# Small constant bf16 products on TensorE inside the attention walks of a graph network

## The chip, the cores and the metric

The kernel runs on one core of one Trainium2 chip. The metric is the device time of one execution in microseconds (us), taken as the median of several executions. The profile is one further execution, recorded by the hardware profiler; its span runs from the first to the last recorded instruction.

## The reference

Four layers run one after the other over 3125 nodes with 256 features, each a graph attention followed by a feed-forward part with experts, each added to `x`. The change touches the graph attention of layer 0, layer 1 and layer 2 (there twice, called l2a and l2b below). All of them compute, over 50,000 edges sorted by target node and with 8 heads:

```
h = einsum('nd,dhf->nhf', x, W)
logits = leaky_relu(al_s[src] + al_d[dst], 0.2)     # al_s, al_d: 8 numbers for each node
m = segment_max(logits, dst)
e = exp(logits - m[dst])
out = segment_sum(h[src] * e, dst) / (segment_sum(e, dst) + eps)
```

In l2a and l2b each node also has an edge to itself. Layer 3's attention and all the feed-forward parts have loops of their own and are not touched.

## The kernel before

`gat_layer` (line 1207) normalizes and transposes the nodes, projects them (`project`), and calls `gat_edges` (line 597), the walk over the edges. It is called four times: l0, l1, l2a, l2b; in the profile's names the digits of l0 and l1 are left out, so that both are `l_edges`.

A walk takes the edges in 416 tiles of 128, in 26 chunks (`NCK`) of 16 tiles (`CK`), each chunk in four groups (`GR` = 4 tiles). For a tile, `stage` holds the gathered rows of the source nodes (256 features, their 8 ones and 8 logits of the source). A product of a one-hot matrix `hotT` with `adn` gives every edge the logits of its target node (the **expansion**, line 856, into `ps_ad`); a product of the one-hot matrix `hot` with the weighted rows `msg` sums the edges of each target node (the **scatter**, line 890, into `ps_sum`), and DVE adds the sum to `acc` (line 764), one tile at a time. The softmax runs with a running maximum: the logits of a chunk are turned (line 863), scanned on DVE, the ends of the tiles and the tops of the chunk are passed through two small products (lines 867 and 872), the maxima are turned back (line 877), and the first block's sums are rescaled (line 753, with the product of line 881).

Each engine has its own program, and semaphores tie them. All of it is software-pipelined: while chunk c is scattered, the maxima of chunk c + 1 are made.

- **POOL** (line 653) issues one indirect gather for a tile. From the third chunk on, a group's gathers wait for `msg_built` of the same group two chunks before, since `stage` has two halves.
- **SP** (line 661) loads the rows for `hotT`.
- **DVE** in a chunk (line 768): `weigh` (line 745, makes `msg` of one group), `rescale`, the logits of the next chunk (lines 677 to 685, which need `ps_ad`), then three times `weigh` and a step of the maxima with four adds between its instructions (lines 691 to 697, 705 to 714, 722 to 730), then `hotT` of chunk c + 2 (line 672), `exponents` (lines 738 and 739, which need the turned maxima) and the last four adds.
- **ACT** makes `hot` (lines 812, 815), the weights (line 828), and in l2a and l2b the own weights (line 820).
- **PE** in a chunk (line 892): scatter of group 0, turn of the logits; scatter 1, `place_ends`; scatter 2, `place_tops`; scatter 3, the block numbers of chunk c + 2 into registers, `turn_maxima`, `place_f`, and the expansion of chunk c + 2. A scatter's product waits until DVE has added what `ps_sum` of the same number held (`added`).

The walk uses the eight PSUM banks: four `ps_sum`, `ps_ad`, `ps_p`, `ps_x` (the turned logits, and in its first columns `ps_f`) and `ps_y` (turned maxima, `ps_ends`, `ps_init`). All of the operands of its products are f32.

## Time and profile before

| | us |
|---|---|
| median of 3 runs | 7869.34 (7864.52 to 7906.43) |
| span of the profiled execution | 7089.8 |
| PE busy | 5426.1 (77%) |
| DVE busy | 4048.3 (57%) |
| POOL busy | 2934.6 (41%) |
| ACT busy | 2394.9 (34%) |
| mean granted TensorE clock | 0.796 of full |

The median lies 779.5 us over the span: that much lies around the first and the last recorded instruction. The busy shares are means over stages with different limits; the walks stand at about 210 to 860, 1500 to 2150, 2520 to 3170 and 3265 to 3920 us of the span.

In the rows below, PE is TensorE's products, PEld its weight loads, which overlap them. A clock of 1.00 is 2.4 GHz and 0.50 is 1.2 GHz. An f32 product appears as two records of each kind, so that 16 expansions are 32 records and the four products of one scatter are 8. A record's own duration includes the time in which it overlaps its neighbours; the pace is read from starts.

### The profile page before, as it was taken

How to read it: one execution, taken by the hardware profiler on the slowest of the kernel's cores; microseconds unless marked ns; L12 is line 12 of the kernel's file. 1: busy time of each engine (PE TensorE's matmuls, PEld its weight loads, DVE VectorE, ACT ScalarE, POOL GpSimd, SP SyncE). 2: the span in 40 equal slices, each digit the busy share in tenths (PEclk: the TensorE clock that was granted, in tenths of full speed). 3: DMA queues.
4: the chain of work that ended last, by engine and by line, in shares of the span. 5: the costliest groups of instructions: out<-in, count | busy, mean ns of one | idle time of the engine just before them, and what ended most of it. 6: DMA issues, size and time to landing. Idle time of an engine off the chain costs nothing. (4 is left out here: it accounts for less than half of the span.)

```text
span 7089.8 us, 85054 instructions
## 1 busy us (share of the span) xinstructions
PE 5426.1 (77%) x21265; PEld 3965.8 (56%) x21266; DVE 4048.3 (57%) x8410; ACT 2394.9 (34%) x5747; POOL 2934.6 (41%) x2894
## 2 busy tenths in 40 slices
PE   0788759458886678875888488888979998476998
PEld 0566436346664555654666344446768887354776
DVE  5466733356664447764777577762147776794112
ACT  0333212123332133332333255542205554362333
POOL 1566432336660056644666277760007776000000
PEclk9666659766667866766766699998989999796999
DMA  3433323233440044433334111110019999461000
GB/s 89 124 115 116 70 79 110 80 93 114 117 103 12 2 123 114 117 93 98 115 115 100 41 30 32 31 19 18 7 48 345 353 357 254 120 196 16 9 13 23
DMA packets 455428, 710.74 MB, mean 100 GB/s; under 512 B 105113, under 2 KB 334039, under 8 KB 455015
## 3 DMA queue, kind: packets, MB, share of 16 engines
q0 software_dynamic: 142432, 380.88, 19.8%
q1 hardware_dynamic: 310442, 318.36, 14.1%
q10 hardware_dynamic: 2304, 8.52, 0.3%
q8 instruction: 114, 1.87, 0.1%
q14 instruction: 136, 1.11, 0.1%
HBM read 604.94 MB, written 102.97 MB: 100 GB/s over the span
## 5 line engine op out<-in xcount | busy, mean ns | idle before, releaser
L653 POOL DMA_INDIRECT l_edges_stage<-l_h_rows,src_t x832 | 831.9, 1000 | 463.5 <-issue 238.9
L890 PE MATMUL l_edges_ps_sum<-l_edges_msg,l_edges_hot 128*128 128x264 f32 x1664 | 741.2, 609 | 172.2 <-DVE l_attn_acc L764 157.1
L2086 POOL DMA_INDIRECT l_edge_kv<-l_kv_rows,src_t x416 | 465.1, 1118 | 741.0 <-POOLq L1999 557.2
L2522 POOL DMA_INDIRECT l_gate_edges_srow<-l_gate_src_rows,l_gate_edges_idx x512 | 567.6, 1109 | 251.4 <-issue 155.8
L890 PEld LDWEIGHTS l_edges_ps_sum<-l_edges_msg,l_edges_hot 128*128 128x128 f32 x1664 | 446.4, 291 | 373.2 <-DVE l_attn_acc L764 276.9
L2656 PE MATMUL l_gate_edges_ps<-l_gate_edges_wide,l_gate_edges_hot_lo 128*128 128x500 f32 x1024 | 487.0, 633 | 127.3 <-DVE l_gate_edges_wide L2584 127.3
L653 POOL DMA_INDIRECT l2a_edges_stage<-l2a_h_rows,src_t x416 | 414.0, 995 | 236.8 <-issue 114.7
L653 POOL DMA_INDIRECT l2b_edges_stage<-l2b_h_rows,src_t x416 | 413.2, 993 | 237.4 <-issue 116.8
L890 PE MATMUL l2b_edges_ps_sum<-l2b_edges_msg,l2b_edges_hot 128*128 128x272 f32 x832 | 355.3, 581 | 87.6 <-DVE l2b_attn_acc L764 79.8
L890 PE MATMUL l2a_edges_ps_sum<-l2a_edges_msg,l2a_edges_hot 128*128 128x272 f32 x832 | 353.9, 579 | 87.6 <-DVE l2a_attn_acc L764 77.7
L2656 PEld LDWEIGHTS l_gate_edges_ps<-l_gate_edges_wide,l_gate_edges_hot_lo 128*128 128x128 f32 x1024 | 204.9, 205 | 369.6 <-issue 214.5
L764 DVE TENSOR_TENSOR l_attn_acc<-l_attn_acc,l_edges_ps_sum 128x264 f32 x832 | 350.4, 421 | 79.4 <-DVE l_attn_acc L764 34.1
L2187 PE MATMUL l_edge_ps_e<-l_edge_w,l_edge_eaT 128*128 128x256 f32 x1664 | 377.0, 380 | 0.0
L2307 DVE SCALAR_TENSOR_TENSOR l3f_acc<-l_experts_psb,l3f_g,l3f_acc 128x256 f32<-128x256 f32 x200 | 96.8, 484 | 444.7 <-PE l_experts_psb L2338 444.6
L2187 PEld LDWEIGHTS l_edge_ps_e<-l_edge_w,l_edge_eaT 128*128 128x128 f32 x1664 | 317.8, 191 | 43.9
L890 PEld LDWEIGHTS l2b_edges_ps_sum<-l2b_edges_msg,l2b_edges_hot 128*128 128x128 f32 x832 | 204.1, 271 | 198.0 <-DVE l2b_attn_acc L764 153.7
L2368 ACT ACTIVATE l_experts_hT<-l_experts_psa,l_experts_sc_pair 128x320 f32<-128x320 f32 x320 | 197.5, 617 | 343.3 <-PE l_experts_psa L2329 323.3
L890 PEld LDWEIGHTS l2a_edges_ps_sum<-l2a_edges_msg,l2a_edges_hot 128*128 128x128 f32 x832 | 201.7, 268 | 198.5 <-DVE l2a_attn_acc L764 155.6
L2584 DVE TENSOR_TENSOR l_gate_edges_wide<-l_gate_edges_hot_hi,l_gate_edges_val 128x500 f32<-128x500 f32 x512 | 307.6, 674 | 6.4
L1133 PE MATMUL l_agg_ps<-l_agg_msg,l_agg_hot 128*128 128x264 f32 x832 | 209.0, 409 | 82.8 <-DVE l_attn_acc L1098 69.2
L856 PE MATMUL l_edges_ps_ad<-l_attn_adn,l_edges_hotT 128*128 x1664 | 250.2, 291 | 28.2 <-DVE l_edges_hotT L672 28.2
L2613 ACT ACTIVATE l_gate_edges_hot_lo<-col,l_gate_edges_nlo 128x128 f32<-128x128 f32 x512 | 156.4, 388 | 338.0 <-PE l_gate_edges_ps L2656 338.0
(745 smaller groups left out, 11376.6 us busy)
## 6 DMA issues: line engine op xcount, KB each, us to landing
l_val_rows<-l_edge_vj SPq DMA_DIRECT2D x104, 512.0 KB, 5.7
l_agg_stage<-l_val_rows SPq DMA_DIRECT2D x52, 1024.0 KB, 5.3
l_edge_ea<-in_edge_attr SPq DMA_DIRECT2D x388, 128.0 KB, 5.1
l_edges_rel_b<-rel_rows SPq DMA_DIRECT2D x52, 512.0 KB, 4.0
l_experts_w<-in_L_ffn_w SPq DMA_DIRECT2D x32, 512.0 KB, 4.6
l_gate_edges_lo_b<-l_gate_edges_lo_rows SPq DMA_DIRECT2D x64, 256.0 KB, 3.2
l_edges_stage<-l_h_rows,src_t POOLq DMA_INDIRECT x832, 2.8
l2a_edges_rel_b<-rel_rows SPq DMA_DIRECT2D x26, 512.0 KB, 4.0
```

The lines of the kernel that those rows point to most:

```text
L653: nc.gpsimd.indirect_dma_start(out=stage[:, c % 2, u, :], out_offset=None, in_=h_rows, in_offset=bass.IndirectOffsetOnAxis(ap=K.src_t[:, c ...
L764: nc.vector.tensor_tensor(to, to, ps_sum[u][:], ALU.add).then_inc(added, 1)
L856: last = nc.tensor.matmul(ps_ad[:, u, :], hotT[:, u * P:(u + 1) * P], adn[:, bass.ds(blks[u], 1), :].rearrange("p a h -> p (a h)"), start= ...
L890: nc.tensor.matmul(ps_sum[u][:], hot[:, g, u, :], msg[:, g % 2, u, :], start=True, stop=True).then_inc(summed, 1)
L1133: nc.tensor.matmul(ps[u][:], hot[:, n % 2, u, :], msg[:, n % 2, u, :], start=True, stop=True).then_inc(summed, 1)
L2086: nc.gpsimd.indirect_dma_start(out=kv[:, m, u, :], out_offset=None, in_=kv_rows, in_offset=bass.IndirectOffsetOnAxis(ap=K.src_t[:, n * EB ...
L2187: last = nc.tensor.matmul(ps_e[h][:, u, :], eaT[:, n % ES, 2 * h + u, c, :], w[:, c, :], start=(c == 0), stop=(c == DC - 1))
L2368: nc.scalar.activation(hT[l][:, v % 2, f, half * HALF:(half + 1) * HALF], psa[n % NA][:], ACT.Relu, bias=sc_pair[:, 1, l, v // NG, f:f + 1 ...
L2522: nc.gpsimd.indirect_dma_start(out=srow[:, n % 4, u, :], out_offset=None, in_=src_rows, in_offset=bass.IndirectOffsetOnAxis(ap=idx[:, n * ...
L2584: nc.vector.tensor_tensor(wide[:, s, u], bcast(hot_hi[:, n % 3, u, :], GV), val[:, s, u, :].unsqueeze(1).to_broadcast([P, NT, GV]), ALU.mu ...
L2613: nc.scalar.activation(hot_lo[:, s, u, :], K.col[:], ACT.Abs, bias=nlo[:, n * GB + u:n * GB + u + 1]).then_inc(near_lo, 1)
L2656: nc.tensor.matmul(flat, hot_lo[:, n % 2, u, :], wide[:, n % 2, u].rearrange("p t f -> p (t f)"), start=False, stop=False).then_inc(summed, 1)
```

## The change

A constant tile `warm` of ones in bf16 (128 x 256) is set once. `keep_warm(n)` issues n products of its first 128 columns with all 256, into a PSUM bank that nobody reads. PE issues two of them ahead of each of the 16 tiles of an expansion, and five after each of the four scatters of a chunk (after the small product that follows the scatter for groups 0 to 2, and ahead of the last small products for group 3). That is 32 + 20 in a chunk. To free a bank, `ps_x` and `ps_y` become one bank `ps_w` with separate columns for all five small results, and `place_f`, whose result no longer lies over the turned logits, goes ahead of `turn_maxima`. No wait is added or removed.

```diff
--- before.py
+++ after.py
@@ -133,6 +133,7 @@
                 nc.gpsimd.iota(col_i[:], [[1, P]], base=0, channel_multiplier=0).then_inc(iota_set, 1)
                 nc.gpsimd.iota(row_i[:], [[1, 1]], base=0, channel_multiplier=1).then_inc(iota_set, 1)
                 nc.gpsimd.memset(K.izero[:], 0).then_inc(ident_set, 1)
+                nc.gpsimd.memset(K.warm[:], 1.0)
 
             @block.vector
             def _(dve):
@@ -491,6 +492,7 @@
         self.ones = sb("ones", [P, P])
         self.col = sb("col", [P, P])
         self.row = sb("row", [P, 1])
+        self.warm = sb("warm", [P, 2 * P], BF16)
         self.izero = sb("izero", [P, BATCH], U32)
         self.rel_t = sb("rel_t", [P, STEPS])
         self.bad_t = sb("bad_t", [P, STEPS])
@@ -629,10 +631,10 @@
         ps_sum = [ph.psum(f"ps_sum{u}", [P, MW]) for u in range(GR)]
         ps_ad = ph.psum("ps_ad", [P, CK, AW])
         ps_p = ph.psum("ps_p", [P, CK, HEADS])
-        ps_x = ph.psum("ps_x", [P, P])
-        ps_y = ph.psum("ps_y", [P, P + 2 * CK + 2])
-        lgT, ps_f = ps_x[:], ps_x[:, 0:HEADS]
-        maxT, ps_ends, ps_init = ps_y[:, 0:P], ps_y[0:HEADS, P:P + 2 * CK], ps_y[:, P + 2 * CK:P + 2 * CK + 2]
+        ps_w = ph.psum("ps_w", [P, 2 * P + 2 * CK + 2 + HEADS])
+        ps_warm = ph.psum("ps_warm", [P, 2 * P])
+        lgT, maxT, ps_ends = ps_w[:, 0:P], ps_w[:, P:2 * P], ps_w[0:HEADS, 2 * P:2 * P + 2 * CK]
+        ps_init, ps_f = ps_w[:, 2 * P + 2 * CK:2 * P + 2 * CK + 2], ps_w[:, 2 * P + 2 * CK + 2:]
 
         rel_in = [ph.sem(f"rel_in{m}") for m in range(2)]
         gathered = [ph.sem(f"gathered{m}") for m in range(2)]
@@ -848,11 +850,16 @@
 
             @block.tensor
             def _(pe):
+                def keep_warm(n):
+                    for _ in range(n):
+                        nc.tensor.matmul(ps_warm[:], K.warm[:, 0:P], K.warm[:], start=True, stop=True)
+
                 def expand(c, m, blks):
                     pe.wait_ge(hotT_built, c + 1)
                     if not (isinstance(c, int) and c == 0):
                         pe.wait_ge(lg_made, c)
                     for u in range(CK):
+                        keep_warm(2)
                         last = nc.tensor.matmul(ps_ad[:, u, :], hotT[:, u * P:(u + 1) * P],
                                                 adn[:, bass.ds(blks[u], 1), :].rearrange("p a h -> p (a h)"), start=True, stop=True)
                     last.then_inc(expanded, 1)
@@ -893,18 +900,22 @@
                     scatter(c, 0)
                     if after >= 1:
                         turn_logits(c + 1, 1 - m)
+                    keep_warm(5)
                     scatter(c, 1)
                     if after >= 1:
                         place_ends(c + 1)
+                    keep_warm(5)
                     scatter(c, 2)
                     if after >= 1:
                         place_tops(c + 1)
+                    keep_warm(5)
                     scatter(c, 3)
                     if after >= 2:
                         blks = block_ids(nc, mybir.EngineType.PE, K, c + 2)
+                    keep_warm(5)
                     if after >= 1:
+                        place_f(c + 1)
                         turn_maxima(c + 1)
-                        place_f(c + 1)
                     if after >= 2:
                         expand(c + 2, m, blks)
 
@@ -913,8 +924,8 @@
                 turn_logits(0, 0)
                 place_ends(0)
                 place_tops(0)
+                place_f(0)
                 turn_maxima(0)
-                place_f(0)
                 expand(1, 1, block_ids(nc, mybir.EngineType.PE, K, 1))
                 with pe.Fori(0, NCK // 2 - 1) as j:
                     for m in range(2):
```

## Rows read from the trace of the kernel before

**Rows 1.** The page's parts 1 and 2: span, PE busy, granted clock

```profile
span 7089.8 us, 85054 instructions
...
PE 5426.1 (77%) x21265; PEld 3965.8 (56%) x21266; DVE 4048.3 (57%) x8410; ACT 2394.9 (34%) x5747; POOL 2934.6 (41%) x2894
...
PEclk9666659766667866766766699998989999796999
```

**Rows 2.** Groups by line: count, busy us, mean ns, idle before

```profile
L890 PE MATMUL l_edges_ps_sum<-l_edges_msg,l_edges_hot 128*128 128x264 f32 x1664 | 741.2, 609 | 172.2 <-DVE l_attn_acc L764 157.1 <-DVE l_edges_msg L745 7.1
...
L653 POOL DMA_INDIRECT l_edges_stage<-l_h_rows,src_t x832 | 831.9, 1000 | 463.5 <-issue 238.9 <-DVE l_edges_msg L745 148.3 <-POOLq L528 76.3
```

**Rows 3.** Line 753 without its first run, in layer 0 and l2a

```profile
L753 DVE SCALAR_TENSOR_TENSOR l_attn_acc<-l_edges_ps_x,l_attn_acc x25: 426/433/434, 274.1 to 845.6; 128x264 f32 x25
...
L753 DVE SCALAR_TENSOR_TENSOR l2a_attn_acc<-l2a_edges_ps_x,l2a_attn_acc x25: 426/433/434, 2583.2 to 3159.9; 128x264 f32 x25
```

**Rows 4.** Gathers: l2a's group by line; landing in layers 0 and 1

```profile
L653 POOL DMA_INDIRECT l2a_edges_stage<-l2a_h_rows,src_t x416 | 414.0, 995 | 236.8 <-issue 114.7 <-DVE l2a_edges_msg L745 84.6 <-POOLq L528 37.5
...
DMA to landing us min/median/max: 2.7/2.8/5.2
```

**Rows 5.** Sum and mean of twelve stretches of 25 us, l2a

```profile
sum 300.00, PE 259.39 PEld 184.80 DVE 217.09 ACT 111.84 POOL 197.55; mean PE 21.62 PEld 15.40 DVE 18.09 ACT 9.32 POOL 16.46
```

**Rows 6.** Stretches of 1 us: busy PE, PEld, DVE, ACT, POOL, PEclk, DMA

```profile
2728.50:2729.50 1.00, 1.00 (x6) 1.00 (x6) 0.00 (x0) 0.00 (x0) 0.69 (x2) 0.50 0.50 139
...
2742.50:2743.50 1.00, 0.21 (x1) 0.21 (x2) 0.86 (x3) 0.00 (x0) 0.70 (x2) 1.00 0.52 139
...
2747.50:2748.50 1.00, 1.00 (x9) 1.00 (x9) 0.79 (x3) 0.76 (x3) 0.76 (x1) 0.78 0.82 262
...
606.90:607.90 1.00, 1.00 (x12) 1.00 (x11) 0.96 (x2) 1.00 (x4) 0.00 (x0) 1.00 0.60 229
...
607.90:608.90 1.00, 1.00 (x7) 1.00 (x7) 0.99 (x2) 0.97 (x3) 0.10 (x1) 0.50 0.01 4
...
615.90:616.90 1.00, 1.00 (x3) 0.77 (x3) 1.00 (x2) 0.00 (x0) 0.69 (x2) 0.50 0.32 83
```

**Rows 7.** Time order, one chunk of l2a: start, us, engine, line, idle before

```profile
2722.77 0.29 DVE L738 TENSOR_TENSOR l2a_edges_own_x<-l2a_edges_own,l2a_edges_ps_y 128x128 f32<-128x128 f32 x1 [0.63 <-PE l2a_edges_ps_y L877]
...
2723.19 7.01 PE L856 MATMUL l2a_edges_ps_ad<-l2a_attn_adn,l2a_edges_hotT 128*128 x32
...
2726.69 0.43 DVE L753 SCALAR_TENSOR_TENSOR l2a_attn_acc<-l2a_edges_ps_x,l2a_attn_acc 128x264 f32 x1
...
2730.03 3.98 PE L890 MATMUL l2a_edges_ps_sum<-l2a_edges_msg,l2a_edges_hot 128*128 128x272 f32 x8
...
2730.34 0.29 DVE L677 TENSOR_TENSOR l2a_edges_z<-l2a_edges_stage,l2a_edges_ps_ad 128x128 f32<-128x128 f32 x1 [3.22 <-PE l2a_edges_ps_ad L856]
...
2734.37 0.42 DVE L691 TENSOR_TENSOR_SCAN l2a_edges_local<-cuts_f,l2a_edges_ps_x 128x128 f32<-128x128 f32 x1 [1.68 <-PE l2a_edges_ps_x L863]
...
2735.17 2.54 PE L890 MATMUL l2a_edges_ps_sum<-l2a_edges_msg,l2a_edges_hot 128*128 128x272 f32 x8 [0.95 <-DVE l2a_attn_acc L764]
...
2743.29 2.88 PE L890 MATMUL l2a_edges_ps_sum<-l2a_edges_msg,l2a_edges_hot 128*128 128x272 f32 x8 [0.81 <-DVE l2a_attn_acc L764]
...
2746.71 0.32 PE L877 MATMUL l2a_edges_ps_y<-ident,l2a_edges_seg_max 128*128 128x128 f32 x1 [0.54 <-issue]
```

**Rows 8.** The same view, one chunk of layer 0

```profile
604.95 4.34 PE L856 MATMUL l_edges_ps_ad<-l_attn_adn,l_edges_hotT 128*128 x32
...
609.14 3.87 PE L890 MATMUL l_edges_ps_sum<-l_edges_msg,l_edges_hot 128*128 128x264 f32 x8
...
613.37 0.42 DVE L691 TENSOR_TENSOR_SCAN l_edges_local<-cuts_f,l_edges_ps_x 128x128 f32<-128x128 f32 x1 [2.17 <-PE l_edges_ps_x L863]
...
628.25 0.34 PE L877 MATMUL l_edges_ps_y<-ident,l_edges_seg_max 128*128 128x128 f32 x1
```

**Rows 9.** Line 856 alone while the clock is full, layer 0

```profile
L856 PE MATMUL l_edges_ps_ad<-l_attn_adn,l_edges_hotT x26: 256/256/277, 604.9 to 607.8; 128*128 x26
```

## The prediction

> **What bounds the kernel now.** I read the page's totals first [rows 1]: the span is 7089.8 us, PE is busy for 77% of it, and its clock line shows 6s and 7s where the attention layers run, so TensorE often has half of its clock there. A sum over 7 ms says nothing about four loops of 600 us, so the next view is the costliest groups [rows 2]: the scatter product (line 890) and the gathers (line 653) of `gat_edges` are at its top, and with the expansion (line 856) they are the work of the four walks. The starts of the one rescaling per chunk (line 753) give their pace [rows 3]: in layer 0, 25 of the 26 lie from 274.1 to 845.6 us, 23.8 us a chunk, and in l2a from 2583.2 to 3159.9, 24.0. The first one is left out: it stands some 32 us before the second, in both, because the first gathers are still being issued. Layer 1 keeps the pace of layer 0, and l2b that of l2a.
>
> Three engines could set that pace. POOL: 416 gathers of l2a take 414 us busy, 114.7 us of issue between them, and 84.6 us in which POOL waits for `msg` [rows 4]. Its own work is therefore (414 + 114.7) / 26 = 20.3 us a chunk. It has some 3.5 us to spare. DVE is busy for 18.1 of every 25 us [rows 5], and waits for PE at three places: for `ps_ad` (3.22 us), for the turned logits (1.68 and 2.17 us) and for the turned maxima (0.63 us) [rows 7, 8]. PE is busy for 21.6 of every 25 us [rows 5]. So the loop is PE and DVE handing work to each other, and in the long hand-overs PE is late.
>
> Now the clock, microsecond by microsecond [rows 6]. In l2a the scatters of groups 1 to 3 run at 1.00 (2.4 GHz), though PE is idle for about 1 us ahead of each (0.95 and 0.81 ahead of the first and the last [rows 7]). The expansion begins half a microsecond after 2746.71 us, and in the microsecond from 2747.5 the mean is down to 0.78 with PE busy 1.00; the level it falls to is 0.50 (1.2 GHz), as in the chunk before. It stays there through expansion and scatter 0, and scatter 1 has the full clock again: 2.54 us against 3.98 [rows 7]. In layer 0 the expansion starts at 1.00, falls at about 607.9 in its midst, and the scatters are mostly at 0.50. What goes before a fall is thus seldom idleness: it is the stretch of expansions, weight loads with products of 8 or 16 columns.
>
> **The change, part by part.** Walk the chunk from one expansion's start to the next, and price it with the full clock everywhere.
>
> (a) Expansion, 16 tiles. In layer 0, 26 records start in 2.8 us at the full clock [rows 9], 0.108 us each, 0.216 a tile of two records; at half clock 32 take 6.9 us, 0.43 a tile [rows 7]. The change puts two bf16 products of 256 columns ahead of each tile. No row shows such a product. One column a cycle gives 256 / 2.4 GHz = 0.107 us, and 0.213 at half clock; that is the low end. The nearest row, a scatter record of 264 or 272 columns in f32, takes 3.98 / 8 = 0.50 us at half clock [rows 7], so 0.25 at full: it passes its columns twice, and is the high end. I take 0.107, since a 16-bit operand has no need of the second pass. If the first f32 weight load lies wholly beside the second of them, a tile costs 0.216 + 0.214 - 0.107 = 0.32 us; if nothing overlaps and their own two loads (half an f32 load each) show too, 0.54. Loads lie beside products in the scatters, but a filler's load behind a tiny product has no cover, so I take 0.40: 6.4 us an expansion, from 5.2 to 8.6. Against 4.34 us (layer 0 [rows 8]) and 6.9 (l2a) that is +2.1 and -0.5 us.
>
> The Trainium skill (TensorE: Matmul & The Clock Gate, section Back-to-back issue gap) states columns / 2.4 GHz plus 2.5 ns, 0.109 us for this product; no run here shows it yet, and by it the sum would be the same within 0.1 us a chunk.
>
> (b) From the expansion's end to the first scan over the turned logits (line 691). In layer 0 that is 609.29 to 613.37 us, in l2a 2730.15 to 2734.37 [rows 7, 8], nearly all of it scatter 0 at half clock (3.87 and 3.98 us) and the turn. At full clock the scatter takes 1.95 us, and the DVE's own work there (line 677 to the end of `weigh`) takes about 2.0 to 2.4, which is next late. The stretch shrinks from 4.1 and 4.2 us to 2.4 and 2.5: -1.7 us in both.
>
> (c) From there to the turn of the maxima (line 877). In l2a at full clock: 2734.37 to 2746.71, 12.34 us, paced by DVE's adds, which PE waits for [rows 7]. In layer 0, mostly at half clock: 613.37 to 628.25, 14.88 us [rows 8]. At full clock layer 0 should fall to the same 12.34: -2.5 us there, 0 in l2a. Three sets of five fillers (0.54 us each) fall into this part, ahead of scatters 1, 2 and 3, where PE is idle for 0.81 us at the least [rows 7]. They cost nothing at full clock; at half clock (1.07 us) they would show by up to 0.3 us each.
>
> (d) The fourth set stands between scatter 3 and the last small products, where nothing covers it: +0.54 us. `place_f` now goes ahead of `turn_maxima`; the two take the same time together, so the expansion starts no later by it, but the DVE's exponents come 0.3 to 0.4 us later. Who waits for that: the last four adds, `weigh` of the next group 0 and through it POOL. From the exponents (line 738, 2722.77) to line 677 (2730.34 less its wait of 3.22) is 4.35 us of DVE work [rows 7], under the 6.4 us of the expansion, so it is covered; without that cover it would be 0.4 us a chunk.
>
> (e) The rest: merging the small results into one PSUM bank adds no wait, since the order of their writers and readers stands; the memset of `warm` is once. The added weight loads and products (52 pairs a chunk) go through PE's queue alone; SP and POOL get nothing.
>
> Sum for a chunk: layers 0 and 1, 2.1 - 1.7 - 2.5 + 0.54 = -1.6 us, to about 22.3; l2a and l2b, -0.5 - 1.7 + 0.54 = -1.7 us, to about 22.4. Times 24 chunks and two walks each: 77 + 82 = 159 us. Against the profiled execution: 7089.8 - 159 = 6931 us of span. The median of the runs, 7869.34, lies 779.5 us over that span; what lies around the span doesn't change, so the forecast is 7869 - 159 = 7710 us, 2.0% less.
>
> What could stop it earlier: POOL. A gather waits for `weigh` of the chunk two before, and the next logits wait for the last gather to land (2.8 us [rows 4]). From line 677 to the end of the following `weigh` would be 2.4 + 12.34 + 1.1 + 3.9 us (the last from 2722.77 to the rescaling at 2726.69 [rows 7]), 19.7 in all; with 3.8 for the last gather and its landing and 15 x 1.27 for the gathers between, two chunks take 42.6 us: 21.3 us is the least for a chunk. 22.3 is above it, but little more is to be had.
>
> **Rivals.** (A) The fillers don't hold the clock through the expansion. For it: it falls there today with PE busy the whole time, and why it falls is only inferred. Against it: what falls is the stretch of tiny products, and the fillers bring 512 columns a tile; scatters with idle gaps between them keep the full clock in l2a. Price, if nothing changes in the clock: in l2a a tile costs 0.80 us, the expansion 12.8 (+5.9), the last fillers 1.07, the gaps 0.4: +7.3 us a chunk. In layer 0, 2.9 us at full clock do seven tiles and nine take 7.0: 9.9 (+5.6), with the rest +7.0. Times 48 each: +690, 8550 us; if the scatters gain the clock and only the expansions lose it, some 8250. I take 8400. The change decides at an expansion of about 6.4 + 1.65 = 8.0 us, 0.50 a tile: dearer than that and it is slower.
>
> The Trainium skill (same page, section HAM oscillation — how this bites in real kernels) ties the fall to idle gaps longer than any within these walks. The trace disagrees: 0.50 with PE busy 1.00 [rows 6]. By that rule fillers in short gaps would change nothing in the clock, and their cost would stay: rival A's 8550 us.
>
> (B) The clock holds, but fillers are dear (about 0.50 us a tile, no overlap, sequencer time for four instruction pairs a tile): expansion 8.0 us, no gain: 7870 us. (C) They are cheap (0.33 a tile) and POOL's 21.3 us becomes the bound: gains of 2.5 and 2.7 us, 48 times each, 250 us: 7620 us.
>
> **How the numbers follow.** Forecast 0.52, (C) 0.16, (B) 0.14, (A) 0.18. The low end is (C) with 20 us to spare, 7600. The high end takes in (B) and the mild edge of (A), 7960; what lies beyond is most of (A), under 2 in 10. A measurement of this kernel can tell 0.5% (39 us) from no change. Faster by more: 0.52 + 0.16 less a little = 0.67; within: 0.13; slower: 0.20.
>
> **What would show it.** Right: the granted clock at 0.9 to 1.0 all through the walks, in the expansions above all; 32 fillers and 32 expansion records in about 6.4 us; scatter 0 in about 2.0 us; line 753 every 22.3 to 22.4 us; POOL's wait for `msg` down from 84.6 us to about 40 in l2a; PE busier, near 0.9. Wrong: the clock still at 0.50 in an expansion, or an expansion over 8 us at full clock, or chunks under 21.3 us.

## The result and the profile after

The change made the kernel slower. Its median is 8166.59 us (8149.32 to 8170.57) beside 7880.51 us (7864.52 to 7906.43) for the kernel before (the runs of the 7869.34 above and one more), a ratio of 1.036 [1.033, 1.040]. The forecast was 7710 us, 2.0% faster, and its range ended at 7960.

The first view is the page of the kernel after: span, busy time of each engine, granted clock in 40 slices (it answers [rows 1]).

```profile
span 8168.8 us, 95871 instructions
...
PE 5570.9 (68%) x26673; PEld 4090.1 (50%) x26674; DVE 4044.2 (50%) x8410; ACT 2391.9 (29%) x5747; POOL 2871.8 (35%) x2895
...
PEclk9787768867787867778677877888898999788899
```

Two things stand in it. This execution's own time was 8170.57 us, so what lies around its span is 1.8 us, not 779.5. And its span is 1079 us over that of the shown profile of before [rows 1], though its clock line is higher (mostly 7s and 8s in the walks, where before has 6s and 7s), DVE, ACT and POOL are busy for as long as they were, and PE for only 145 us more. The time went into waiting, and far more of it than the two medians are apart.

The costliest groups (instruction count, busy us, mean ns, then the idle time before them and what ended it; they answer [rows 2, 4]):

```profile
L655 POOL DMA_INDIRECT l_edges_stage<-l_h_rows,src_t x832 | 818.6, 984 | 937.0 <-DVE l_edges_msg L747 630.3
L897 PE MATMUL l_edges_ps_sum<-l_edges_msg,l_edges_hot 128*128 128x264 f32 x1664 | 593.9, 503 | 539.0 <-DVE l_attn_acc L766 457.9
...
L655 POOL DMA_INDIRECT l2a_edges_stage<-l2a_h_rows,src_t x416 | 402.6, 968 | 488.3 <-DVE l2a_edges_msg L747 336.9
...
L855 PE MATMUL l_edges_ps_warm<-warm 128*128 128x256 bf16 x2704 | 475.2, 284 | 41.0 <-DVE l_edges_hotT L674 28.7
```

The scatters of layers 0 and 1 take 594 us of PE where they took 741 [rows 2]: the clock gain is there. But POOL, which was to wait 40 us for `msg` in l2a, waits 337 us. The pace of the rescaling in layer 0 (line 755, which was 753; the columns are as in [rows 3]) shows how much slower the loop turns:

```profile
L755 DVE SCALAR_TENSOR_TENSOR l_attn_acc<-l_edges_ps_w,l_attn_acc x25: 427/432/434, 302.7 to 1075.5; 128x264 f32 x25
```

That is 772.8 us for 24 chunks, 32.2 us each, against 23.8 [rows 3] and a forecast of 22.3. The waits of DVE and POOL in the walk of l2a name the place (who <- what it waited for: us in total, times, longest us):

```profile
POOL l2a_edges_stage L655 <- DVE l2a_edges_msg L747: 336.9, 46, 14.7
DVE l2a_edges_run L707 <- remote: 202.0, 22, 10.0
...
DVE l2a_edges_init L724 <- remote: 33.1, 4, 8.9
```

26 times in this walk, once a chunk, DVE waits for something that the profile can't name ("remote"), for 9.0 us on average and 8.5 to 10 us in 22 of them. Lines 707 and 724 read the small PSUM results that PE wrote, so it is PE they wait for. The time order of one such place (start, us, engine, line, idle before):

```profile
3258.84 0.23 PE L874 MATMUL l2a_edges_ps_w<-l2a_edges_placed,of_head 128*8 128x32 f32 x2
...
3259.00 0.72 PE L855 MATMUL l2a_edges_ps_warm<-warm 128*128 128x256 bf16 x5
3259.45 0.95 POOL L655 DMA_INDIRECT l2a_edges_stage<-l2a_h_rows,src_t  x1 [0.30 <-issue]
...
3265.72 0.95 POOL L655 DMA_INDIRECT l2a_edges_stage<-l2a_h_rows,src_t  x1 [0.30 <-issue]
3269.13 0.23 ACT L822 ACTIVATE l2a_edges_msg<-l2a_edges_own_x 128x32 f32<-128x32 f32 x1 [11.91 <-DMA pair_rows<-l0f_acc,l0f_slot]
3269.29 0.27 DVE L707 TENSOR_TENSOR_SCAN l2a_edges_run<-links_f,l2a_edges_top,l2a_edges_ps_w 8x32 f32<-8x32 f32 x1 [9.99 <-remote]
```

The product that DVE needs is recorded as done at 3259.07 us. DVE uses it at 3269.29. ACT, which by the program waits for the scatter ahead of it (the DMA in its bracket belongs to another stage), goes on at the same moment. Between them nothing works but POOL, which issues the six gathers that it may still issue; 3.5 us after the start of the last one both engines go on together. I call this a hold-up. The shown trace of before has none: its longest wait of DVE for PE in these walks is the 3.22 us of [rows 7].

It is PE's signal that comes late, and not DVE that is slow to take it. The trace also records when a semaphore is raised. The one that line 874 raises is recorded at 3269.15 us here, 10.1 us after the product's end; the four scatter products ahead of it, done from 3257.1 to 3258.9, have theirs at 3262.71, 3265.58, 3267.00 and 3269.11, so the signals come through one by one while POOL issues. In the kernel after, 90 of the 104 signals of line 874 are recorded over 1 us late (median of these 9.3 us), and DVE starts within 0.2 us of the late one. In x0_before, in the shown trace of before and in the runs with plain transfers below, all 104 stand 0.01 us behind the product's end. Some such records are missing in the traces with hold-ups.

### The profile page after: what moved, and what is told of

Its sections match the earlier page's. It is cut to its first block and busy times, and to the rows that moved or that the text cites. A ratio compares the mean times of both kernels' runs of the same rounds, so it can differ in the third digit from the quotient of the medians.

```text
span 8168.8 us, 95871 instructions
## 1 busy us (share of the span) xinstructions
PE 5570.9 (68%) x26673; PEld 4090.1 (50%) x26674; DVE 4044.2 (50%) x8410; ACT 2391.9 (29%) x5747; POOL 2871.8 (35%) x2895
## 5 line engine op out<-in xcount | busy, mean ns | idle before, releaser
L897 PE MATMUL l_edges_ps_sum<-l_edges_msg,l_edges_hot 128*128 128x264 f32 x1664 | 593.9, 503 | 539.0 <-DVE l_attn_acc L766 457.9
L2097 POOL DMA_INDIRECT l_edge_kv<-l_kv_rows,src_t x416 | 434.2, 1044 | 875.5 <-POOLq L2010 559.1
L897 PEld LDWEIGHTS l_edges_ps_sum<-l_edges_msg,l_edges_hot 128*128 128x128 f32 x1664 | 353.9, 238 | 723.0 <-DVE l_attn_acc L766 561.5
L855 PE MATMUL l_edges_ps_warm<-warm 128*128 128x256 bf16 x2704 | 475.2, 284 | 41.0 <-DVE l_edges_hotT L674 28.7
L897 PE MATMUL l2a_edges_ps_sum<-l2a_edges_msg,l2a_edges_hot 128*128 128x272 f32 x832 | 303.1, 511 | 277.5 <-DVE l2a_attn_acc L766 258.5
L897 PE MATMUL l2b_edges_ps_sum<-l2b_edges_msg,l2b_edges_hot 128*128 128x272 f32 x832 | 300.7, 506 | 266.0 <-DVE l2b_attn_acc L766 222.8
L897 PEld LDWEIGHTS l2a_edges_ps_sum<-l2a_edges_msg,l2a_edges_hot 128*128 128x128 f32 x832 | 177.0, 238 | 373.7 <-DVE l2a_attn_acc L766 308.0
L897 PEld LDWEIGHTS l2b_edges_ps_sum<-l2b_edges_msg,l2b_edges_hot 128*128 128x128 f32 x832 | 173.3, 234 | 363.8 <-DVE l2b_attn_acc L766 276.5
L855 PEld LDWEIGHTS l_edges_ps_warm<-warm 128*128 128x128 bf16 x2704 | 276.7, 127 | 81.9 <-issue 30.1
L863 PEld LDWEIGHTS l_edges_ps_ad<-l_attn_adn,l_edges_hotT 128*128 128x128 f32 x1664 | 265.4, 201 | 14.4 <-issue 0.6
```

Source lines behind the costliest of these rows:

```text
L855: nc.tensor.matmul(ps_warm[:], K.warm[:, 0:P], K.warm[:], start=True, stop=True)
L863: last = nc.tensor.matmul(ps_ad[:, u, :], hotT[:, u * P:(u + 1) * P], adn[:, bass.ds(blks[u], 1), :].rearrange("p a h -> p (a h)"), start= ...
L897: nc.tensor.matmul(ps_sum[u][:], hot[:, g, u, :], msg[:, g % 2, u, :], start=True, stop=True).then_inc(summed, 1)
L2097: nc.gpsimd.indirect_dma_start(out=kv[:, m, u, :], out_offset=None, in_=kv_rows, in_offset=bass.IndirectOffsetOnAxis(ap=K.src_t[:, n * EB ...
```

## The experiments

The runs came in six sets, each on one chip, each beside the kernel before on the same chip. Three theories stood against each other:

- **Fillers too dear** or the clock not held (rivals B and A of the prediction): then the loss is there whatever POOL does.
- **Hold-ups**: PE's signals reach DVE and ACT late while POOL issues indirect gathers; the runs of before have this too, its shown trace has not, and the change makes it worse.
- **Bank and order**: putting the small results into one PSUM bank, or turning the maxima after the factors, costs time by itself.

All kernels of the experiments load PE's 65 register values of the `need` table one by one, and not in groups:

```diff
-    loaded(mybir.EngineType.PE, plan.need, i, ...)
+    [pe.value_load(plan.need[0:1, k:k + 1], ...) ...]
```

What that costs is measured by x0_before and x1_before, the kernel before with this edit alone.

> The kernel before once more (the block needs of layer 0's experts are read one by one, 65 loads in place of 5 groups, which should cost under 10 us). It is to settle where the 779.5 us between the span of its profile (7089.8 us) and its timed runs (7869) lie. Theory 1: inside the walks; the timed runs hold a stall in each looped chunk as the changed kernel's trace does (9.9 us, before line 707 of DVE), and the profile shown had none: then this run's profile has a span near 7870 us and chunks of about 31 us. Rival: outside the first and last instruction: then the span is near 7090 and the chunks take 24 us, as before.

> The kernel before again with the single loads, for the trace of these runs' chip: 7118 us and chunks of 24 us if this chip behaves as the last one did; 7870 us or more and chunks of about 31 us with a stall if it behaves as in the first comparison, and then the trace shows where.

x0_before: 7117.6 us beside 7087.89, 1.0039 [1.0025, 1.0054]. x1_before, on another chip: 7760.75 beside 7743.65, 1.0033 [1.0008, 1.0058]. The edit costs 17 to 30 us, not under 10. The finding is the other number: the same kernel takes 7088 us on one chip and 7744 on another. Line 753 of the one and of the other, in layer 0:

```profile
L753 DVE SCALAR_TENSOR_TENSOR l_attn_acc<-l_edges_ps_x,l_attn_acc x25: 427/433/434, 273.6 to 848.7; 128x264 f32 x25
```

```profile
L753 DVE SCALAR_TENSOR_TENSOR l_attn_acc<-l_edges_ps_x,l_attn_acc x25: 423/433/433, 283.8 to 979.9; 128x264 f32 x25
```

23.96 us a chunk in x0_before, 29.0 in x1_before. From first to last rescaling the four walks (layer 0, layer 1, l2a, l2b) take 606, 603, 606 and 609 us in x0_before and 738, 743, 736 and 749 in x1_before: 542 of the 632 us between the two spans. x1_before has hold-ups as the kernel after has; one of them in time order:

```profile
380.49 0.72 PE L872 MATMUL l_edges_ps_y<-ones,l_edges_spread 8*128 8x1 f32 x4
...
384.97 0.95 POOL L653 DMA_INDIRECT l_edges_stage<-l_h_rows,src_t  x1 [0.31 <-issue]
388.49 0.16 DVE L722 COPY l_edges_init<-l_edges_ps_y 128x2 f32<-128x2 f32 x1 [7.54 <-remote]
```

Again 3.5 us from the last gather's start, but that is no rule. By the hold-ups of over 2.5 us in the last 24 chunks of layer 0, DVE goes on 3.4 to 4.1 us after the start of POOL's latest gather in the kernel after and in h1_after; in e4_after, the same kernel on another chip, it is 0.3 to 3.8 us (median 2.0), in x1_before from 0.3 to 3.8 and in h3_after_paced 0.5 to 2.8, and in e6_wide 20 of 40 end while POOL goes on issuing. So the kernel before has hold-ups where it takes 7744 us or more, without any filler, and none where it takes 7088. Of the six chips of the experiments four were of the first kind (before at 7744, 7763, 7864 and 7877 us), two of the second (7088 and 7095). On each chip all runs of before agreed within 1%. The shown trace of before, with a span of 7089.8, is of the second kind; its timed runs, 7864 to 7906, have no trace, but by their time are of the first. Whether the two ran on one chip isn't known, so "chip" stands here for whatever stays the same within one set of runs.

**The change without hold-ups, in parts** (chip with before at 7088 us).

```diff
@@ e1_no_fillers
-                        keep_warm(2)
+                        keep_warm(0)
...
-                    keep_warm(5)        (all four)
+                    keep_warm(0)
@@ e2_only_expand
-                    keep_warm(5)        (all four)
+                    keep_warm(0)
@@ e3_only_groups and e7_groups_again
-                        keep_warm(2)
+                        keep_warm(0)
```

> The changed kernel without any filler: one bank for the small results and place_f ahead of turn_maxima, nothing else. If the stall comes from the fillers (or their number of instructions): ratio 0.99 to 1.01 to the kernel before. If it comes from the merged bank (PE writes and DVE reads in one bank): the chunks keep a stall of about 9.9 us and the ratio is 1.03 or more.

> Only the 32 fillers in each expansion; none at the groups. If the cost follows the count of PE instructions in a loop body: about 32/52 of the loss, ratio near 1.02, with the stall later in the chunk. If it is the fillers at the groups (behind place_ends and place_tops) that hold back the signals: no stall, ratio 0.97 to 0.99, since the expansion keeps the full clock (my step a).

> Only the 20 fillers at the groups of a chunk; none in the expansion. If the count of instructions decides: 20/52 of the loss, ratio near 1.01. If fillers behind place_ends and place_tops hold back the signals: the stall of 9.9 us stays before line 707 and the ratio is 1.04 or more, since nothing is gained in the expansion, whose clock falls as before.

> Only the 20 fillers at the groups, beside the others. On a chip with stalls: if PE being quicker is what makes the stalls longer (POOL is always behind and issues without a pause), this one is slower than before too, ratio 1.02 to 1.04; if the dense products in the expansion do it, 1.00. On a chip without: 0.985 again.

e1: 7132.66 us, 1.0057 [1.0040, 1.0075], 15 us over x0_before with the same clock (0.793 and 0.795 over the span): bank and order bring nothing and cost about 0.2% where there are no hold-ups; no run tells what they do where there are. e2: 7020.52 us, 0.9906 [0.9889, 0.9924], 97 us under x0_before. e3: 6983.78 us, 0.9852 [0.9835, 0.9868], 134 us under it. e7 repeats e3 on the second chip of this kind: 6984.79 beside 7094.6, 0.9851 [0.9834, 0.9869]. Either half of the fillers is a gain here; the fillers at the groups alone bring the larger part.

In e2 the products of the expansion don't always hold the clock. This is an expansion in layer 0 that began at half clock. First two stretches of 2 us within it (length, busy PE, PEld, DVE, ACT, POOL, granted clock, DMA), then its last tile and the DVE behind it:

```profile
373.00:375.00 2.00, 2.00 (x14) 1.81 (x12) 1.51 (x4) 1.47 (x5) 1.64 (x2) 0.50 0.92 300
380.00:382.00 2.00, 2.00 (x15) 1.81 (x15) 0.00 (x0) 0.00 (x0) 1.39 (x3) 0.50 0.37 107
```

```profile
382.87 0.59 PE L855 MATMUL l_edges_ps_warm<-warm 128*128 128x256 bf16 x2
383.25 0.43 PE L863 MATMUL l_edges_ps_ad<-l_attn_adn,l_edges_hotT 128*128 x2
383.53 2.99 PE L897 MATMUL l_edges_ps_sum<-l_edges_msg,l_edges_hot 128*128 128x264 f32 x6
383.81 0.29 DVE L679 TENSOR_TENSOR l_edges_z<-l_edges_stage,l_edges_ps_ad 128x128 f32<-128x128 f32 x1 [6.04 <-PE l_edges_ps_ad L863]
```

From 372.82 to 383.53 it takes 10.7 us, 0.67 a tile, at 0.50 with PE busy all the time, and the DVE waits 6.0 us at its end. That is rival A, in one chunk of each three to seven. In layer 0 these chunks take 28 to 29.4 us, the others 20.2 to 21.5. Of the 104 expansions of e2 27 began at 0.50 and stayed there (10.4 us each), and 77 began at 1.00 and kept it (5.7 us each): the 512 filler columns a tile held the clock that they found and didn't bring it back. (In h1_after, below, three of eleven that began at 0.50 did run at full clock.) The fillers at the groups, which keep the full clock up to the expansion's start, are what the complete change has more.

**The complete change and its variants, with hold-ups** (before at 7744 us). One filler a tile in e5; in e6 fillers of 512 columns, one a tile and three at a group.

```diff
@@ e5_one_per_tile
-                        keep_warm(2)
+                        keep_warm(1)
@@ e6_wide
-        self.warm = sb("warm", [P, 2 * P], BF16)
+        self.warm = sb("warm", [P, 4 * P], BF16)
-        ps_warm = ph.psum("ps_warm", [P, 2 * P])
+        ps_warm = ph.psum("ps_warm", [P, 4 * P])
-                        keep_warm(2)
+                        keep_warm(1)
-                    keep_warm(5)        (all four)
+                    keep_warm(3)
```

> The changed kernel itself, with the 65 single loads that the other experiments have (28 us of cost by the first one). Theory 1: the change gains in the chunks (each half of the fillers alone gave 0.985 and 0.991), and what made it slow in the first comparison is a stall of 9 to 10 us in each looped chunk that belongs to the runs there, not to the kernel's own work: its chunks here take 20.5 to 21.5 us and the ratio is 0.965 to 0.975. Rival: the stall of 9.9 us comes with all 52 fillers together (a number of instructions in the loop body that 32 or 20 stay under): chunks of 33 us and a ratio of 1.12 or more here.

> One filler per tile in the expansion in place of two, five at each group. If half of the columns hold the clock through the expansion: 0.36 us a tile falls to about 0.25, but the gathers (20.3 us a chunk) are then the bound: the ratio is that of the full change or 0.005 better. If the clock falls in the expansions again: ratio 0.975 to 0.985, near that of fillers at the groups alone (0.985).

> The same columns in half the instructions: one product of 512 columns per tile, three at each group (28 fillers a chunk in place of 52). If a stall follows the number of PE instructions, it is shorter or gone where the full change has it; if columns and time alone count, the ratio is that of the full change within 0.005.

e4: 8006.78 us, 1.0345 [1.0314, 1.0376]. e5: 8101.77, 1.0468 [1.0436, 1.0501]. e6: 8078.5, 1.0442 [1.0405, 1.0479]. The result comes back on this chip, and fewer or fewer but wider fillers are worse. To add up hold-ups I count each idle time of DVE over 1.5 us at whose end the awaited product had stood recorded as done for over 1 us. In the last 24 chunks of layer 0 they sum to 129 us in x1_before (24 of them), 183 in e4 (23), 244 in e5 (29) and 243 in e6 (40): the two slower variants are held up longer. This alone does not tell whether the hold-ups are a cause or a companion.

**Pacing POOL.** If the length of a hold-up is set by the gathers that POOL may still issue, a wait ahead of each gather shortens it. It costs time of its own.

```diff
@@ f1_after_paced, f2_before_paced, h3_after_paced
+                            if c >= 2:
+                                pool.wait_ge(added, (c - 2) * CK + u + 1 + GR)
```

> The changed kernel, with POOL made to follow DVE more closely: each gather also waits until the tile of the same place two chunks before has been added. Theory 2: on a chip where the kernel before takes 7740 us or more, PE's signals are held up while POOL issues gathers, and come through about 3.5 us after POOL's last one (median 3.51 us in the changed kernel's trace, 26 stalls); here POOL runs out of permitted gathers sooner, so a stall is 4 to 6 us instead of 9 to 10, chunks of 26 to 29 us instead of 32 to 33, and the ratio is 0.95 to 0.99 there. Rival: the hold-up has nothing to do with POOL: stalls and chunks stay as they were (ratio 1.035 there). On a chip without stalls both give 0.97 to 0.99.

> The kernel before with the same closer pacing of the gathers. Theory 2: on a chip with stalls its chunks fall from 27 to 32 us to 25 to 28, ratio 0.96 to 0.98; without stalls 1.00 to 1.02. Rival: 1.00 to 1.01 on either.

> The changed kernel with the closer pacing of POOL again. On a chip without stalls 1.039, as before. On a chip with stalls: theory 2 says that each stall is cut short, since POOL runs out of permitted gathers after one to four instead of five to nine: stalls of 4 to 6 us, chunks of 27 to 30 us, and a time under the changed kernel's own there (7600 to 7850 us); the rival, that a stall lasts its 9 us whatever POOL may issue, says 8100 us or more.

f1 and f2 fell on a chip without hold-ups, where there was nothing to shorten: 7371.72 us, 1.0393 [1.0376, 1.0411], and 7389.09 us, 1.0419 [1.0402, 1.0437]. They say only that the pacing costs the kernel before 294 us (17 to 30 of them by the single loads), and that the change gains next to nothing under it. h3, on a chip with hold-ups (before 7877.19): 8060.23 us, 1.0229 [1.0188, 1.0269], 128 us less than the same kernel without pacing (h1_after, below), though the pacing costs time of its own: in layer 0's walk the DVE waits 122.8 us for expansions where it waits 45.1 in h1. The 7600 to 7850 us expected left that out. By the same count its hold-ups in layer 0 are 26 with 108 us, 2 to 5 us each with two or three gathers in them, where h1 has 26 with 215 us, most of them of 8.5 to 10 us with five. The waits of DVE in that walk of h3 and then of h1:

```profile
DVE l_edges_init L726 <- remote: 87.7, 21, 5.2
...
DVE l_edges_x L743 <- remote: 24.9, 6, 4.9
```

```profile
DVE l_edges_run L707 <- remote: 181.7, 21, 9.9
...
DVE l_edges_init L724 <- remote: 38.1, 4, 10.1
```

The longest falls from 9.9 and 10.1 to 5.2 us. The length of a hold-up does go with POOL's gathers.

**No indirect gathers.** The stage is filled by plain transfers of the same size through the same queue. They read rows in order and not by index, so what is aggregated is other data. POOL's part changes in two ways at once: there is no index, and a transfer keeps it busy for 0.54 us and not for 1.0 (l2a of h2 and of before). These runs don't tell the two apart.

```diff
@@ f3_after_direct, g2_after_direct, h2_before_direct
-                            nc.gpsimd.indirect_dma_start(out=stage[:, c % 2, u, :], ..., in_=h_rows, ...)
+                            k = (c * CK + u) % NT
+                            pool.dma_start(stage[:, c % 2, u, :], h_rows[k * P:(k + 1) * P, :]).then_inc(gathered[c % 2], 16)
```

> The changed kernel with the same bytes fetched by plain transfers of 128 rows in a row in place of the indirect gathers (so the edges get wrong source rows): POOL has next to nothing to issue. Theory 2: no stalls on any chip, chunks of 20.0 us, bound by DVE and PE, the kernel near 6700 us. Rival (PE's own signals are slow when it runs dense products, whatever POOL does): stalls of 9 us stay on a chip that has them.

> The changed kernel once more, beside the kernel before. If this chip is one without stalls (before near 7090 us): the gains of the halves (0.985 and 0.991) mostly add up, chunks of 20.5 to 21.5 us, ratio 0.965 to 0.975. If the rival holds, that all 52 fillers in one loop body make the stall by themselves, it shows here: chunks of 33 us, ratio 1.12 or more. On a chip with stalls (before 7740 or more): 1.035 as before.

> The changed kernel with plain transfers in place of the indirect gathers (the edges get wrong source rows), on whatever chip this is. On a chip without stalls 0.969 again. On a chip with stalls: theory 2 (the hold-up belongs to POOL's issuing of gathers) says no stalls and 6880 to 7000 us, far under the kernel before there (ratio 0.90 or less); the rival (PE's dense products alone) says chunks near 30 us and 1.0 or more.

> The changed kernel beside the kernel before, for a chip without stalls (before near 7090 us), where it has not been seen yet: chunks of 20.5 to 21.5 us and 0.965 to 0.975 if the gains of the two halves mostly add up; 1.00 or more, with stalls, if the full set makes stalls by itself. On a chip with stalls 1.028 to 1.036 once more.

> The kernel before with plain transfers in place of the indirect gathers (the edges get wrong source rows). It tells what the fillers alone do where nothing is held up: the changed kernel without gathers took 6876 us beside a before of 7095, and 6961 beside 7763. If the fillers are worth what steps (a) to (d) say, this one takes 150 to 250 us more than that: 7050 to 7100 on a chip without stalls, 7100 to 7200 on one with, in chunks of 23.5 to 24 us and no stalls. If they are worth nothing: 6880 and 6960.

f3, without hold-ups (before 7094.6): 6876.26 us, 0.9693 [0.9676, 0.9709]. On a chip with hold-ups (before 7763.19) the change is 7982.09, 1.0277 [1.0233, 1.0320] (g1), and with plain transfers 6960.8, 0.8956 [0.8922, 0.8990] (g2). On another (before 7877.19) it is 8188.22, 1.0398 [1.0358, 1.0437] (h1), and the kernel **before** with plain transfers is 7196.41, 0.9140 [0.9105, 0.9175] (h2). Neither g2 nor h2 has a wait of the kind left in any of the four walks. Outside them, where the other indirect transfers stayed, g2 still has some (ACT waits 110.7 us in 14 such waits at line 2154), and f3, on a chip without hold-ups, has none; that is where g2's 85 us over f3 lie, for the walks of the two are alike. The rescalings of layer 0 without their first, in g2 and then in h2:

```profile
L755 DVE SCALAR_TENSOR_TENSOR l_attn_acc<-l_edges_ps_w,l_attn_acc x25: 427/433/434, 272.7 to 784.2; 128x264 f32 x25
```

```profile
L753 DVE SCALAR_TENSOR_TENSOR l_attn_acc<-l_edges_ps_x,l_attn_acc x25: 427/433/434, 259.9 to 832.4; 128x264 f32 x25
```

21.3 us a chunk (511.5 / 24) against 23.9 (572.5 / 24). h2 has the pace of the shown trace of before and of x0_before (23.8 and 24.0), which have indirect gathers and no hold-ups. So plain transfers don't make this loop faster; they take away the hold-ups alone. And with the hold-ups gone the change is worth 2.5 us a chunk in layer 0. From first to last rescaling the four walks of h2 take 599 us each, those of g2 542, 542, 551 and 550: 212 us for the whole change (the two ran on different chips; f3, on a third, has g2's times in all four).

The waits of DVE in these 24 chunks show what the change does where nothing is held up. h2, then g2:

```profile
DVE l_edges_local L691 <- PE l_edges_ps_x L863: 52.1, 24, 2.2
DVE l_edges_run L705 <- PE l_edges_ps_y L867: 29.0, 23, 1.3
DVE l_edges_init L722 <- PE l_edges_ps_y L872: 24.7, 24, 1.3
DVE l_edges_x L739 <- PE l_edges_ps_y L877: 16.7, 24, 0.9
...
DVE l_edges_z L677 <- PE l_edges_ps_ad L856: 12.9, 14, 3.3
```

```profile
DVE l_edges_x L741 <- PE l_edges_ps_w L884: 35.0, 24, 1.9
DVE l_edges_z L679 <- PE l_edges_ps_ad L863: 31.8, 24, 1.6
...
DVE l_edges_local L693 <- PE l_edges_ps_w L870: 5.5, 24, 0.2
DVE l_edges_init L724 <- PE l_edges_ps_w L879: 4.1, 24, 0.2
```

The waits behind scatters (the first three rows of h2, 106 us) shrink to 10 us; those for the expansion and for the turned maxima grow from 30 to 67 us, by the fillers in the expansion and by the last five. Net 59 us of the walk's 61.

**Tiny fillers.** Do PE's many instructions lengthen the hold-ups, whatever is in them? i1 keeps their number and makes each 8 by 8.

```diff
@@ i1_tiny
-                        nc.tensor.matmul(ps_warm[:], K.warm[:, 0:P], K.warm[:], start=True, stop=True)
+                        nc.tensor.matmul(ps_warm[0:8, 0:8], K.warm[:, 0:8], K.warm[:, 0:8], start=True, stop=True)
```

> The changed kernel with the same 52 added products per chunk, each of 8 columns and 8 weights in place of 256 and 128: the instructions and their records stay, the array has next to nothing to do, and the clock should fall in the expansions as in the kernel before. On a chip with stalls: if the loss comes with the number of PE instructions, stalls of 9 us in nearly every looped chunk and a ratio of 1.03 or more; if it comes with PE being quicker (POOL then always has gathers owed and never pauses), stalls as in the kernel before and 1.00 to 1.02. On a chip without stalls: 1.00 to 1.02 with the clock of before (mean near 0.79), which says that the 0.985 and 0.991 of the halves came with the columns and the clock.

8301.74 us beside 7863.93, 1.0567 [1.0525, 1.0608], the worst of all. Its hold-ups in layer 0 come to 138 us (23), near x1_before's 129 and under e4's 183; over all four walks they are 650 us, against 469 in x1_before, 799 in e4 and 876 in h1. The same number of PE instructions thus goes with shorter hold-ups than in the complete change. Whether it lengthens them over the kernel before stays open, since that has no trace on i1's chip. What i1 loses most by is its expansions. In the one at 647.6 us of layer 0 a tile takes 0.44 us at the full clock, more than with two wide fillers (0.36, below) and twice the kernel before's (0.22 [rows 9]), and 0.65 us after the clock has gone to 0.50 in its midst, at 650 us. In 24 chunks of layer 0 the DVE waits 119 us for expansions (line 679) against 37 in h1. That is 3.4 us a chunk; were it so in all 104 chunks it would be 355 us by this estimate, the larger part of the 438 that i1 is over before.

## Why the prediction was wrong

**The base failed, not the sum of parts.** The prediction put "the median of the runs, 7869.34, ... 779.5 us over that span" down to what lies around the span and said that this "doesn't change". In every run here 1.8 us or so lie around the span (x0_before: 7125.4 within 7127.22; the kernel after: 8168.8 within 8170.57). The timed runs of before have no trace of their own; between the two traces of it that differ as they do, x0_before and x1_before, 542 of 632 us lie inside the walks, where PE's signals are held up. A term for this stands nowhere in the sum, which put it at nothing, and no rival names it. All that I read of the walks, waits above all, was read from a loop that the timed runs, by their time, don't turn. On such a chip the change didn't take 1.6 us off a chunk of layer 0 but added 1.8 (x1_before to e4, below). Where nothing is held up the parts (a) to (d) come out near what I took; I read them from the waits of h2 and g2, 24 chunks of layer 0.

**(a) The expansion** was sized a little too dear. In the kernel after, two tiles' worth and the scatter that follows the expansion:

```profile
3213.51 0.38 PE L855 MATMUL l2a_edges_ps_warm<-warm 128*128 128x256 bf16 x2
...
3213.73 0.29 PE L863 MATMUL l2a_edges_ps_ad<-l2a_attn_adn,l2a_edges_hotT 128*128 x2
3213.88 0.38 PE L855 MATMUL l2a_edges_ps_warm<-warm 128*128 128x256 bf16 x2
...
3219.24 2.08 PE L897 MATMUL l2a_edges_ps_sum<-l2a_edges_msg,l2a_edges_hot 128*128 128x272 f32 x8
```

From 3213.51 to 3219.24 it is 5.7 us, 0.36 a tile; I took 0.40 and 6.4 us. The DVE's wait for it grows by 0.8 us a chunk (12.9 to 31.8 us), where I had 2.1. The granted clock was 1.00 through it:

```profile
3214.00:3216.00 2.00, 2.00 (x25) 1.94 (x23) 1.43 (x5) 1.74 (x7) 0.00 (x0) 1.00 0.34 121
3217.00:3219.00 2.00, 2.00 (x26) 1.92 (x25) 1.06 (x2) 1.60 (x4) 0.95 (x1) 1.00 0.00 0
```

A filler costs what I took: five in 0.72 us and two in 0.38 are 0.113 us apart. The Trainium skill (TensorE: Matmul & The Clock Gate, Back-to-back issue gap) gives 0.109 us for these columns at the full clock, and the trace agrees within 0.004 us. (In (a) I also misread [rows 9]: 26 starts in 2.8 us are 25 steps, 0.225 us a tile and not 0.216; it moves only the low end.)

**(b) Scatter 0** takes 2.08 us where it took 3.98 [rows 7]; I had 1.95. The wait behind it falls by 1.9 us a chunk (52.1 to 5.5 us), where I had 1.7. **(c)** The waits behind the later scatters fall by 2.1 us (29.0 and 24.7 to 4.1 us), where I had 2.5. **(d)** The last fillers and the new order cost what they should: the wait for the turned maxima grows by 0.8 us a chunk (16.7 to 35.0 us), where I had 0.54 and 0.3 to 0.4. Together 2.5 us a chunk in layer 0 (forecast 1.6), 2.0 in l2a (forecast 1.7), and 212 us in all (forecast 159); most of what is missing is (a), put too dear.

**POOL's floor** was put too high: 21.3 us by the sum, but e2's undisturbed chunks in layer 0 alternate between 20.2 and 21.2, 20.7 on average, with DVE waiting in many of them for the last gather; POOL's own work is 20.3 [rows 4]. Rival C's bound is that low, and g2, at 21.3 us with a POOL that has time to spare, doesn't reach it.

**Rival A** is real in parts: it decides e2's bad chunks and has a share in i1. In the complete change 96 of the 104 expansions ran at full clock (the kernel after, and g2 and f3 alike); the other 8 are the first two of each walk, which have no fillers at groups ahead of them. The Trainium skill (same page, HAM oscillation — how this bites in real kernels) ties a lost clock to idle TensorE. The trace of e2 shows a case beside that rule (0.50 with PE busy 2.00 of 2.00, and no way back), that of the hold-ups agrees:

```profile
3260.00:3265.00 5.00, 0.00 (x0) 0.00 (x0) 0.00 (x0) 0.00 (x0) 3.78 (x5) 0.86 0.38 107
3264.00:3268.00 4.00, 0.00 (x0) 0.00 (x0) 0.00 (x0) 0.00 (x0) 2.06 (x3) 0.50 0.42 121
```

PE is idle, and the clock goes from full to 0.50 before the hold-up ends.

**Why slower, and not merely less fast.** Compare x1_before with e4, on one chip, over the last 24 chunks of layer 0: 696.1 and 738.1 us, 1.8 us more a chunk where the change takes off 2.5 without hold-ups. DVE's waits, summed over all rows of the view and with the hold-ups counted as above, tell where. The view's own names won't do for this: 15 waits of x1_before have no releaser in it because a record of a signal is missing, and are as long as their named neighbours, as here:

```profile
DVE l_edges_local L691 <- PE l_edges_ps_x L863: 35.4, 17, 2.2
...
DVE l_edges_local L691 <- issue: 15.0, 7, 2.2
```

| 24 chunks of layer 0, us | h2 (none held) | g2 (none held) | x1_before (held) | e4 (held) |
|---|---|---|---|---|
| walk | 572.5 | 511.5 | 696.1 | 738.1 |
| DVE in hold-ups | 0 | 0 | 128.9 | 183.0 |
| DVE's other waits | 156.3 | 97.4 | 155.2 | 137.1 |

The hold-ups grow by 54 us: there are no more of them (23 against 24), but each takes 8.0 us on average and not 5.4. Over 24 chunks of each of the four walks they grow from 469 to 799 us. In e4 20 of the 23 begin at line 707, earlier in the chunk than line 722 where x1_before has 13. And the other waits, which should fall by 59 us, fall by 18: a hold-up leaves the clock at 0.50, and the scatter behind it runs at half clock again (in e4 the DVE waits 31.1 us for it at line 724, in g2 4.1), while the fillers' cost stays (72 us for the expansion and the turned maxima in e4, 67 in g2). In the kernel after one can see the lost clock at the first scatter behind a hold-up:

```profile
3202.82 4.00 PE L897 MATMUL l2a_edges_ps_sum<-l2a_edges_msg,l2a_edges_hot 128*128 128x272 f32 x8 [10.71 <-DVE l2a_attn_acc L766]
```

4.00 us, the duration of [rows 7] at half clock, behind 10.71 us idle. The four walks take 203 of the 251 us by which e4's span is over that of x1_before.

**What stays open.** Why some chips hold PE's signals while POOL issues indirect gathers and others don't, by what path, and whether it is the index or the longer work of POOL that does it: no run looked there. Why the hold-ups of the complete change begin earlier, and why those of e5 and e6 are longer still; neither the count of fillers nor their columns puts the variants in order. What the one bank and the new order of the small products do to the hold-ups, since e1 had none. The complete change with its own gathers was not run on a chip without hold-ups; its gain there is inferred from its halves (0.991, 0.985) and from the version with plain transfers (0.969).

## What to carry to other kernels

Before a sum is built on a profile, hold the profiled execution's span against the timed median: a rest of 10% is no overhead, it is time that the shown trace doesn't have, and a forecast needs the case in which it sits inside the loop. A change that fills an engine's time is worth what it shows beside the engines that share its chunk: here the same fillers take 2 to 3% off where PE's signals arrive at once (ratios 0.896 / 0.914 = 0.98, and 0.969 for f3) and add 2.8 to 4.0% where they are held up while POOL issues indirect gathers. Clock fillers paid here with 256 columns and not with 8 (which ran only on a chip with hold-ups), and those that stand ahead of the stretch to protect brought more than those within it.

## What the runs showed of the hardware that was not expected

- One kernel with the same inputs took 7088 us on one chip and 7877 on another, 11% apart, with runs on each chip within 1%.
- On four of six chips, signals of TensorE reached VectorE and ScalarE late while GpSimd issued indirect gathers, about once a chunk: in the kernel after 9.3 us (median of the 90 late ones of 104 at line 874), five of them one by one within 10 us. Plain transfers through the same queue didn't do it (7763 to 6961 us with the change, 7877 to 7196 without).
- TensorE went on at 0.50 of its clock for a whole expansion with 512 columns of bf16 a tile in it and no idle time (27 of 104 in e2), and at 1.00 through the same instructions where it had entered them at the full clock (the other 77, and 96 of 104 in the kernel after).
- At the full clock a tile of an expansion took 0.44 us with two fillers of 8 columns ahead of it (i1) and 0.36 us with two of 256.
- The granted clock fell to 0.50 within an idle stretch of 10 us.
